# Four heads in 32-row tiles of one operand instead of zero-padded 128-row operands, in the second attention of a four-stage kernel

## The reference, cut to what matters

```python
mixed_q, mixed_k, mixed_v = x @ wq + bq, x @ wk + bk, x @ wv + bv
c = tanh(mixed_q @ wfq + bfq + (mean(mixed_q) @ wfg + bfg))      # per head
P = sigmoid(sum(c * up)) * 512;  Z = sigmoid(sum(c * uz)) * 512  # centre, width
G = -(j - P) ** 2 * 2.0 / Z ** 2                                 # j: key position
scores = einsum("bhqd,bhkd->bhqk", q, k) / sqrt(8) + G
ctx = softmax(scores) @ v
x = layernorm(x + ctx @ wo + bo)
```

## Time and profile before

| what | value |
|---|---|
| device time, median of 3 runs | 1879.25 us (1878.12 to 1879.94) |
| the profiled execution: span from its first to its last instruction | 1879.1 us |
| its time against the median | 0.15 us apart: practically nothing lies around the span |
| second attention | about 1180 to 1724 us of the span |
| busy over the span | PE 80%, DVE 75%, ACT 59%, POOL 43% |

### The profile page before, as it was taken

One profiled execution on the slowest core, in us unless ns is written; L12 is line 12 of the kernel. 1 busy time (PEld: TensorE's weight loads), 2 busy tenths in 40 slices (PEclk: granted clock), 3 DMA queues, 4 the chain that ended last, 5 costly groups with the idle time before them and its releaser, 6 DMA issues. The chain is left out here.

```text
span 1879.1 us, 38979 instructions
## 1 busy us (share of the span) xinstructions
PE 1509.9 (80%) x12261; PEld 876.3 (47%) x12261; DVE 1402.7 (75%) x3338; ACT 1115.0 (59%) x2433; POOL 800.5 (43%) x1161
## 2 busy tenths in 40 slices
PE   5898889899888989889678988389989998997050
PEld 3566656566565656656445656123233323323050
DVE  4788888888888888888768888377777777784115
ACT  2877767777777877777524444156666666665010
POOL 3655555555555555555435555212112211100626
PEclk8999999999999999999859999599999999998575
DMA  5000000000000000000000000410001000100117
GB/s 164 7 0 1 0 1 0 0 0 0 0 0 0 0 0 0 0 0 0 0 1 1 0 0 0 126 35 29 26 31 34 27 28 29 34 11 16 27 32 74
DMA packets 38862, 34.55 MB, mean 18 GB/s; under 512 B 6124, under 2 KB 35042, under 8 KB 38690
## 3 DMA queue, kind: packets, MB, share of 16 engines
q1 hardware_dynamic: 34946, 28.07, 5.0%
q0 software_dynamic: 2048, 2.77, 1.7%
q10 hardware_dynamic: 1824, 3.15, 0.5%
HBM read 22.43 MB, written 12.85 MB: 19 GB/s over the span
## 5 line engine op out<-in xcount | busy, mean ns | idle before, releaser
L1495 DVE TENSOR_REDUCE a_nm<-a_s 128x1 f16<-128x512 f32 x512 | 324.2, 687 | 59.8 <-PE a_s L1306 58.9
L1426 ACT ACTIVATE a_pt<-a_st 128x1024 f32<-128x1024 f32 x256 | 260.7, 1021 | 116.2 <-PE a_st L1324 112.6
L537 ACT ACTIVATE prob<-score_ps,nmax 128x512 f32<-128x512 f32 (+3 forms) x512 | 266.8, 529 | 19.0 <-DVE nmax L608 19.0
L608 DVE TENSOR_REDUCE nmax<-score_ps 128x1 f32<-128x512 f32 (+3 forms) x512 | 221.1, 483 | 66.1 <-PE score_ps L439 61.3
L129 POOL TENSOR_TENSOR gate<-mhalf 128x1 f32<-128x1 f32 (+1 forms) x276 | 53.2, 193 | 460.5 <-PE score_ps L439 187.2
L453 PE MATMUL pt_ps<-ident,prob 128*128 128x128 f32 x1280 | 192.1, 281 | 70.6 <-DVE pt_l L633 65.4
L633 DVE TENSOR_TENSOR pt_l<-pt_ps,pt_h 128x512 f16<-128x512 f32 (+1 forms) x384 | 223.8, 596 | 32.9 <-ACT pt_h L547 25.8
L1306 PE MATMUL a_s<-a_kop,a_qop 128*128 128x512 f16 x512 | 198.5, 389 | 54.5 <-DVE a_nm L1495 37.3
L547 ACT ACTIVATE pt_h<-pt_ps 128x512 f16<-128x512 f32 (+1 forms) x384 | 204.4, 533 | 58.0 <-PE pt_ps L453 51.2
L453 PEld LDWEIGHTS pt_ps<-ident,prob 128*128 128x128 f32 x1280 | 135.9, 141 | 117.1 <-DVE pt_l L633 107.8
L436 PE MATMUL score_ps<-k_h,q_h 128*128 128x512 f16 (+3 forms) x512 | 155.3, 303 | 11.0 <-issue 10.0
(11 more groups left out here) (350 smaller groups left out, 3742.2 us busy)
## 6 DMA issues: line engine op xcount, KB each, us to landing
a_qop<-q_parts SPq DMA_DIRECT2D x32, 128.0 KB
a_kop<-k_parts SPq DMA_DIRECT2D x128, 24.0 KB
x_tok<-in_L_attn_input_dram SPq DMA_DIRECT2D x4, 512.0 KB, 12.6
e_w<-in_L_ffn_w_dram SPq DMA_DIRECT2D x1, 2048.0 KB, 8.6
q_parts<-a_q_h SPq DMA_DIRECT2D x16, 128.0 KB
k_parts<-a_k_h SPq DMA_DIRECT2D x16, 128.0 KB
out_dram<-c_res SPq DMA_DIRECT2D x8, 256.0 KB
w_raw<-in_L_attn_qkv_dram ACTq DMA_DIRECT2D x1, 1536.0 KB, 7.9
```

Source lines behind the costliest of these rows:

```text
L537: ins = nc.scalar.activation(prob[h][:, P_OFF[c]:P_OFF[c] + w], score_ps[u][:, col:col + w], ACT.Exp, bias=nmax[h][:, c:c + 1], accum_out= ...
L608: ins = nc.vector.tensor_reduce(nmax[h][:, c:c + 1], score_ps[u][:, col:col + P * (c + 1)], AX.X, ALU.max, negate=True)
L1426: nc.scalar.activation(pt[kc % 2][r][:, :, :], st_ps[r][:, :, :], ACT.Exp, scale=1.0 / SC).then_inc(exp_done[r], 1)
L1495: nc.vector.tensor_reduce(nm[g % 2][:, c, hh:hh + 1], s_ps[c % 2][:, :], AX.X, ALU.max, negate=True).then_inc(max_done[c % 2], 1)
```

## The change

Every head of a group gets 32 contiguous rows of its own, 32·hh to 32·hh+31, in `qop[:, g]` and in `kop[:, g]`. The zero padding goes away, and `kop` is a quarter of its size. A head's product runs over the head's 32 rows alone, that is in one of TensorE's four row groups. `head_rows` is that slice.

- **Head scores.** A slot is no longer one head with its four query chunks. It is two heads with two query chunks, one chunk in each half: slots s = 0, 1 of a group take heads 0 and 1, s = 2, 3 take heads 2 and 3. The two head scores of a half come from two row groups and go into the two banks, and stand directly behind each other.
- **Transposed scores.** Half 0 takes heads 0 and 1, half 1 heads 2 and 3, as before, but each from its own row group. They stand behind both head scores of the half.
- **Loads.** `q_parts` and `k_parts` are laid out by head (`(H1, 4, D1, S)`), with the constant key rows written once into `k_parts` by one DMA. A group takes two loads of 128 rows, one for `qop` and one for `kop`, instead of five. The clearing of `kop` (and the semaphore `kzero`) goes away. The minus maxima go to the rows 31, 63, 95 and 127.
- **Weights.** Since the features need no reordering, `wfq`, `wfg`, `bq` and `bk` come in one load each instead of four, and GpSimd splits `wq` and `wk` without a permutation.

```diff
-                for g in range(4):
-                    load(dst[32 * g:32 * g + 32, :], io[f"L1_attn_{name}"].rearrange("(g h d) n -> g d h n", h=4, d=D1)[g])
-            for k, name in enumerate(("bq", "bk")):
-                for g in range(4):
-                    load(m.a_cols[32 * g:32 * g + 32, k:k + 1],
-                         io[f"L1_attn_{name}"].rearrange("(g h d a) -> g d h a", h=4, d=D1, a=1)[g], scattered=True)
-            for k, name in enumerate(("bfq", "bfg")):
-                load(m.a_cols[:, 2 + k:3 + k], io[f"L1_attn_{name}"].rearrange("(p a) -> p a", a=1))
+                load(dst[:, :], io[f"L1_attn_{name}"])
+            for k, name in enumerate(("bq", "bk", "bfq", "bfg")):
...
-        coef = sb("a_coef", [P, QC, G, 8, G], F16)
+        coef = sb("a_coef", [P, QC, G, G, 8], F16)
         qop = sb("a_qop", [P, G, S], F16)
-        kop = sb("a_kop", [P, G, G, S], F16)
+        kop = sb("a_kop", [P, G, S], F16)
...
-        OP_LOADS = (1 + G) * 16
+        OP_LOADS = 2 * 16
...
-        q_dram = nc.dram_tensor("q_parts", (4, 32, G, S), F16).ap()
-        k_dram = nc.dram_tensor("k_parts", (3, 32, G, S), F16).ap()
+        q_dram = nc.dram_tensor("q_parts", (H1, 4, D1, S), F16).ap()
+        k_dram = nc.dram_tensor("k_parts", (H1, 4, D1, S), F16).ap()
...
+        head_rows = lambda hh: slice(32 * hh, 32 * hh + 32)
...
-                sp.wait_ge(kzero, 1)
-                for hh in range(G):
-
-                    sp.dma_start(kop[96 + hh:P:G, hh, :, :],
-                                 io["c_key_rows"].unsqueeze(1).to_broadcast([8, G, S])).then_inc(kconst, 16)
-                sp.wait_ge(kconst, 16 * G)
+                sp.dma_start(k_dram[:, 3, :, :], io["c_key_rows"].unsqueeze(0).to_broadcast([H1, D1, S])).then_inc(kconst, 16)
+                sp.wait_ge(kconst, 16)
...
-                    sp.dma_start(q_dram[n].rearrange("r g n -> g r n"), src[:, :]).then_inc(parts_out, 16)
+                    sp.dma_start(q_dram[:, n, :, :], src[:, :]).then_inc(parts_out, 16)
...
-                    sp.dma_start(k_dram[n].rearrange("r g n -> g r n"), src[:, :]).then_inc(parts_out, 16)
+                    sp.dma_start(k_dram[:, n, :, :], src[:, :]).then_inc(parts_out, 16)
...
-                sp.dma_start(qop[:, g, :], q_dram[:, :, g, :].rearrange("t r n -> (t r) n")).then_inc(op_in[g], 16)
-                for hh in range(G):
-                    sp.dma_start(kop[hh:96:G, hh, g, :],
-                                 k_dram.rearrange("t (d h) g n -> (t d) h g n", h=G)[:, hh, g, :]).then_inc(op_in[g], 16)
+                for rows, parts in ((qop, q_dram), (kop, k_dram)):
+                    sp.dma_start(rows[:, g, :], parts[G * g:G * g + G].rearrange("h t d n -> (h t d) n")).then_inc(op_in[g], 16)
...
-                sp.dma_start(qop[P - G:P, g, :], nm_t[g % 2][:, :]).then_inc(nm_in[g], 16)
+                sp.dma_start(qop[31:P:32, g, :], nm_t[g % 2][:, :]).then_inc(nm_in[g], 16)
...
-            def head_scores(b, g, hh, c):
-
-                if hh == 0 and c == 0:
+            def head_scores(b, g, s, half):
+
+                if s == 0 and half == 0:
                     pe.wait_ge(op_in[g], OP_LOADS * (b + 1))
-                k = c % 2
-                pe.wait_ge(max_done[k], 2 * (16 * b + 4 * g + hh) + c // 2)
-                nc.tensor.matmul(s_ps[k][:, :], qop[:, g, c * P:(c + 1) * P], kop[:, hh, g, :], start=True,
-                                 stop=True).then_inc(s_mm[k], 1)
+                c = 2 * (s % 2) + half
+                for k in range(2):
+                    r = head_rows(2 * (s // 2) + k)
+                    pe.wait_ge(max_done[k], 2 * (16 * b + 4 * g + s) + half)
+                    nc.tensor.matmul(s_ps[k][:, :], qop[r, g, c * P:(c + 1) * P], kop[r, g, :], start=True,
+                                     stop=True).then_inc(s_mm[k], 1)
 
             def scores(half, head, unit):
 
 
-                for c in range(2 * half, 2 * half + 2):
-                    if head:
-                        head_scores(*head, c)
-                    if not unit:
-                        continue
+                if head:
+                    head_scores(*head, half)
+                if unit:
                     b, g, kc, first = unit
-                    if c == 0 and kc == 0:
+                    if half == 0 and kc == 0:
                         pe.wait_ge(nm_in[g], 16 * (b + 1))
-                    if c % 2 == 0:
-                        r = c // 2
-                        pe.wait_ge(exp_done[r], 16 * b + 4 * g + kc)
-                        for i in range(2):
-                            mm = nc.tensor.matmul(st_ps[r][:, i, :], kop[:, 2 * r + i, g, kc * P:(kc + 1) * P], qop[:, g, :],
-                                                  start=True, stop=True)
-                        mm.then_inc(st_mm[r], 1)
+                    pe.wait_ge(exp_done[half], 16 * b + 4 * g + kc)
+                    for i in range(2):
+                        r = head_rows(2 * half + i)
+                        mm = nc.tensor.matmul(st_ps[half][:, i, :], kop[r, g, kc * P:(kc + 1) * P], qop[r, g, :],
+                                              start=True, stop=True)
+                    mm.then_inc(st_mm[half], 1)
...
-                nc.vector.memset(kop[:, :, :, :].rearrange("p a b n -> p (a b n)"), 0.0).then_inc(kzero, 1)
-                nc.vector.memset(coef[:, :, :, :, :].rearrange("p c g t h -> p (c g t h)"), 0.0)
+                nc.vector.memset(coef[:, :, :, :, :].rearrange("p c g h t -> p (c g h t)"), 0.0)
...
             def maxima(half, head, unit):
                 if not head:
                     return
-                b, g, hh = head
-                n = 16 * b + 4 * g + hh
-                if hh == 0 and half == 0:
+                b, g, s = head
+                n = 16 * b + 4 * g + s
+                if s == 0 and half == 0:
 
                     dve.wait_ge(nm_in[(g + 2) % G], 16 * (b + 1) if g >= 2 else 16 * b)
-                for c in range(2 * half, 2 * half + 2):
-                    dve.wait_ge(s_mm[c % 2], 2 * n + c // 2 + 1)
-                    nc.vector.tensor_reduce(nm[g % 2][:, c, hh:hh + 1], s_ps[c % 2][:, :], AX.X, ALU.max,
-                                            negate=True).then_inc(max_done[c % 2], 1)
+                c = 2 * (s % 2) + half
+                for k in range(2):
+                    hh = 2 * (s // 2) + k
+                    dve.wait_ge(s_mm[k], 2 * n + half + 1)
+                    nc.vector.tensor_reduce(nm[g % 2][:, c, hh:hh + 1], s_ps[k][:, :], AX.X, ALU.max,
+                                            negate=True).then_inc(max_done[k], 1)
```

More of the change, by code:

```diff
@@ L372, in _, with load @@
             loads = 0
-            def load(dst, src, scattered=False):
+            def load(dst, src):
                 nonlocal loads
-                sp.dma_start(dst, src, allow_slow_non_contiguous=scattered).then_inc(m.a_loaded, 16)
+                sp.dma_start(dst, src).then_inc(m.a_loaded, 16)
                 loads += 16
@@ L381, in _ @@
             for dst, name in ((m.a_w[:, 3, :], "wfq"), (m.a_wfg[:, :], "wfg")):
-                for g in range(4):
-                    load(dst[32 * g:32 * g + 32, :], io[f"L1_attn_{name}"].rearrange("(g h d) n -> g d h n", h=4, d=D1)[g])
-            for k, name in enumerate(("bq", "bk")):
-                for g in range(4):
-                    load(m.a_cols[32 * g:32 * g + 32, k:k + 1],
-                         io[f"L1_attn_{name}"].rearrange("(g h d a) -> g d h a", h=4, d=D1, a=1)[g], scattered=True)
-            for k, name in enumerate(("bfq", "bfg")):
-                load(m.a_cols[:, 2 + k:3 + k], io[f"L1_attn_{name}"].rearrange("(p a) -> p a", a=1))
+                load(dst[:, :], io[f"L1_attn_{name}"])
+            for k, name in enumerate(("bq", "bk", "bfq", "bfg")):
+                load(m.a_cols[:, k:k + 1], io[f"L1_attn_{name}"].rearrange("(p a) -> p a", a=1))
             for k, name in enumerate(("up", "uz")):
@@ L1020, in _ @@
             for k in range(5):
-                raw, hi, lo = (t[:, k, :] for t in (m.a_w, m.a_w_h, m.a_w_l))
-                if k < 2:
-                    raw = raw.rearrange("p (g h d) -> p g d h", g=4, h=4)
-                    hi, lo = (t.rearrange("p (g d h) -> p g d h", g=4, h=4) for t in (hi, lo))
-                matrices.append((raw, hi, lo))
+                matrices.append(tuple(t[:, k, :] for t in (m.a_w, m.a_w_h, m.a_w_l)))
             for raw, hi, lo in matrices:
@@ L1089, in gauss_attention_phase @@
         names = lambda *a: [sem("a_" + n) for n in a]
-        setup_done, kzero, kconst, vset = names("setup_done", "kzero", "kconst", "vset")
+        setup_done, kconst, vset = names("setup_done", "kconst", "vset")
         misc_mm, misc_out = names("misc_mm", "misc_out")
@@ L1200, in spread @@
                 for n, src in ((0, q_h), (1, q_h), (2, q_l)):
-                    sp.dma_start(q_dram[n].rearrange("r g n -> g r n"), src[:, :]).then_inc(parts_out, 16)
```

(15 more changed lines are left out.)

## The result

The changed kernel took 1983.9 us (median of 4 runs, 1973.0 to 1993.5) against 1879.2 before: a ratio of 1.056, 95% interval 1.051 to 1.061. It is slower, by the mechanism that I named, and by more than the range of 1870 to 1965 held. The profiled execution has a span of 1991.7 us, 112.6 more than before. Two of the kernels further down, pad64 and tiles_old_order, ran in a shorter and a longer group of executions (1902 to 1908 and 1949 to 1962 us; 1921 to 1928 and 1953 to 1955): their ratios go by the shorter group, their profiles are of the longest execution.

What follows compares the result with a forecast made beforehand. The prediction took a loop through TensorE's head scores and VectorE's reduces to bound the kernel. From 1879.1 us, -3.9 for the start, +11 for order and switches and +32 for the clock gave 1918 us, range 1870 to 1965.

Steps and rivals of the forecast that it cites:

- the mechanism that I named: Steady slots: 32-row scores let TensorE's clock fall in spells; likeliest case, chance 0.45, 1895 to 1960 us.
- What bounds the kernel: Each slot: a loop through TensorE and VectorE sets the pace, second half's scores at 1.18 and 1.80 us.
- "faster" rival: Slots: TensorE's freed time, 0.88 us less work each, shortens the slot; 1863 to 1875 us, chance 0.15.
- Transposed scores behind the second head score: Half 1, slots s = 2, 3: `value` comes 0.19 us later, at 2.33; +1.3 us a batch.
- Switches: Extras Q, K, GB, F and CF: changing tile form before the next scores costs about 0.09 each, +0.5 us a batch.
- Middle extras: Slots with nm0 to nm2: second half starts 0.11 us earlier, -0.3 us a batch; CT and OUT give nothing.
- order and switch terms: Steady slots: transposed-score order, tile-form switches and middle extras sum to +1.5 us a batch, +11 us.
- Start: Stage start: no clearing of `kop` saves 1.6 us, fewer `kop` loads 2.3; together -3.9 us.
- bound of -7: Stage start: largest saving, if the writes to `q_parts` had been held up by each other.
- The clock, the step that failed: Steady slots: clock falls about once a batch, about 20 of 122 slots low at +1.6 us each, +32 us.

Runs made afterwards that it cites:

- pad64: Old kernel with the contraction of head scores and transposed scores cut from 128 rows to the first 64; 1907.5 us, ratio 1.013.
- tiles_old_order: Changed kernel with its row tiles, operands and loads, but the old order and pairing of the scores; 1928.5 us over all five executions, ratio 1.022.
- padded_both: Changed kernel's score order in both halves, but with the old zero-padded 128-row operands, nothing side by side; 1914.2 us, ratio 1.018.
- half0full: Changed kernel with the two head scores of half 0 contracting over all 128 rows instead of 32; 1896.8 us, ratio 1.009.
- filler: Changed kernel plus two extra 128-row matmuls ahead of half 0's transposed scores, which then overwrite them; 1907.3 us, ratio 1.013.
- parts_rows: Old kernel with only the scratch tensors q_parts and k_parts reordered to part, group, row; 1876.5 us, ratio 0.998.
- padded: Old kernel's 128-row scores and order with zero-padded kop, but the changed operands and scratch layout, and kop's clearing moved behind a_xt_l; 1872.7 us, ratio 0.996.

## Why the prediction was wrong in size

The direction and the mechanism were right; the step that failed is the count of the slots at the low clock, the last point below.

- **What bounds the kernel:** right. Second half at 1.18 and 1.78 (forecast 1.18 and 1.80), VectorE's reduces 0.6 apart, TensorE's freed time buys nothing in slots without extras. The "faster" rival is out: the padded order alone (padded_both) and the tiles (tiles_old_order) show nothing like 0.88 us a slot.
- **Transposed scores behind the second head score:** mechanism and size right. `value` at 2.31 in s = 3 (2.33), slot 3 longer by 0.16 (0.19).
- **Switches:** right. With 128-row scores next, K, F and GB cost 0.10, 0.10 and 0.08 less (half0full 3.73, 3.95 and 3.53; changed 3.83, 4.05 and 3.61), where I had 0.09. The Trainium skill, "TensorEngine Tiling (Array Packing)", Key Properties, has such a drain at every change of mode; these rows agree, and most of the others are hidden.
- **Middle extras:** too small. Slots 4 and 8 gained 0.15 each, and slots 0, 1, 9, 12, 13 and 15 some 0.05 each, which I had at nothing. At the full clock a batch of changed slots adds up to 63.1 us (slots 2 and 11, which never ran so in the changed kernel, taken from filler: 4.04 and 3.69) against 62.3. So the order and switch terms together are +0.75 us a batch, +6 in all, instead of +11.
- **Start:** -8.0 instead of -3.9. I had taken the writes to end as late as before; the bound of -7 had named the other case ("if they were held up by each other"), and even that was 1 us short. The memory traffic after the last write was issued, in 40 slices, first of the old kernel from 1203 to 1215 us, then of the changed one from 1202 to 1207.5:

```profile
DMA  2222222222222222222222000003542102011123
GB/s 85 92 85 92 96 85 96 96 96 96 96 102 96 99 96 99 96 96 96 96 96 79 17 0 0 0 0 106 174 140 62 38 7 72 3 48 34 10 62 96
```

```profile
DMA  9872000005898200000000003578767688993998
GB/s 231 261 253 90 0 0 0 0 0 149 201 276 261 67 0 0 0 0 0 0 0 0 0 0 119 186 268 298 268 216 276 201 253 283 343 201 67 343 395 291
```

  Before, two tenths of the 16 DMA engines were busy at 96 GB/s for 6.6 us: some 630 KB, nearly five writes of 128 KB. So the writes were a queue that still had to drain; now they move at up to 276 GB/s. The Trainium skill, "DMA: Bandwidth & Descriptors", Why a DMA increments its semaphore by 16 and not by 1, has a DMA run on the largest number of engines up to 16 that divides the outermost dimension of both sides: by it 4 for the old scratch, 16 for the new. The digit 2 (4 of 16 is 0.25) and parts_rows, whose last write landed 1.7 us after its issue, agree.
- **The clock, the step that failed.** I wrote: "I expect the clock to fall about once a batch near XT or PZ and OUT, and to come back with the dense 128-row extras Q, K, F or V, two or three slots later: about 20 of 122 slots." The price of a low slot was right: 1.6 forecast, 4.82 - 3.30 = 1.52 and 5.44 - 3.86 = 1.58 measured. Their number was not: with each slot counted by the share of it that ran at 1.2 GHz, 74 of the 128 slots were low, against 3 before. The clock fell about three times a batch: behind GB, at slot 10 (OUT) and in slot 14. At OUT I had expected it. Behind GB the longest wait of TensorE since the clock had risen was 0.79 us, as in any slot; slot 14 has no extra, though V ahead of it had left a wait of 1.1 us. And it did not come back two or three slots later. The prediction counted Q among what raises it; in the batches 1 to 6 it rose with Q once and with XT once, and otherwise with K in slot 5, with or right behind F in slot 7, or at slot 12 (behind CF or with ctx0). One spell from slot 14 to K, and the stretch between K and the fall behind GB:

```profile
1269.00:1309.00 40.00, 35.91 (x148) 7.24 (x141) 19.68 (x33) 18.47 (x23) 4.04 (x6) 0.50 0.05 14
1309.50:1312.50 3.00, 2.06 (x14) 0.51 (x14) 2.46 (x4) 2.22 (x3) 1.91 (x3) 1.00 0.01 3
```

  No slot without an extra raised the clock here, so a spell that begins in slot 14 lasts up to eight slots. I had counted the falls that gaps cause, when a slot of 32-row scores is itself too light to hold the clock or to raise it. My row for it was also less clean than I read it: the 32-row stretch of the second stage had one pause of 0.63 us, after its transposes.

The account, by slots: the six middle batches took 478.8 us against 373.9 before, 104.9 more. Of that 6 x 0.75 = 4.5 is order and switches; the other 100.4 fall on 61 low slots, 1.65 each. The first batch adds 13.5 and the last 3.0, mostly low slots too, and the start takes 8.0: together 113.4, against 112.6 in the span.

## What to carry to other kernels

Packing the small contractions into row tiles about halved TensorE's work on the scores here, and the clock went with it; where another engine sets the pace, as VectorE does in this loop, the first was worth nothing and the second cost 5%. Before cutting rows, ask what the slot does at 1.2 GHz, and whether a slot without extras could raise the clock again; two 128-row matmuls placed where TensorE waits anyway bought back most of it here. Zero padding that costs no time on the path is not waste: the fastest version here, padded, kept it.

## What was not expected of the hardware

- The clock followed the rows of a matmul, although TensorE was no less busy: 128, 64 and 32 rows gave 1.00, 0.87 (in the longest execution) and 0.67 with TensorE busy 91, 94 and 97%.
- The order of the dimensions of a scratch tensor made the same write three times as slow to land: 6.7 against 2.2 us.
- A load into 32 neighbouring partitions, from one piece of the scratch, was issued in 0.46 us (padded); one of 24 rows into every fourth partition, from rows in steps, in 0.76.
